# A graph network's edge loops: TensorE's sums wait for VectorE's use of the newest product

## The reference, cut to what matters

```python
# L0, convolution (node_h, w1, we, ...)
h = node_h @ w1.T + b1
msg = silu(h[src] + (edge_attr @ we.T + be))
agg = segment_sum(msg, dst, num_segments=N)
...
# L2, heads
score = einsum('ehd,ehd->eh', K[src], Q[dst]) / sqrt(D)     # clipped to -5..5
ex = exp(score - smax[dst]); denom = segment_sum(ex, dst)
m = V[src] * (ex / denom[dst])[:, :, None]
wV = segment_sum(m, dst, num_segments=n)
```

## Time and profile before

| | us |
|---|---|
| median of 3 runs | 6399.58 (6374.36 to 6405.38) |
| profiled execution, its own time | 6349.92 |
| its span | 6348.1 |
| convolution loop in the span | 88 to 1415 |
| heads loop in the span | 3266 to 4680 |
| mean granted clock of TensorE, whole span | 0.731 of 2.4 GHz |

### The profile page before, as it was taken

How to read it: one execution, slowest core, us unless ns; L and a number is a source line. 1 busy time by engine, 2 the same in 40 slices (tenths; PEclk the granted TensorE clock), 3 DMA queues, 4 the chain that set the end, 5 groups by cost and what they waited for, 6 DMA issues and landing times. The chain is left out here.

```text
span 6348.1 us, 91535 instructions
## 1 busy us (share of the span) xinstructions
PE 4079.3 (64%) x19917; PEld 3572.8 (56%) x19918; DVE 2966.6 (47%) x8050; ACT 1654.5 (26%) x2996; POOL 3411.3 (54%) x3536
## 2 busy tenths in 40 slices
PE   4444444456888787787854344444458888878887
PEld 3444444445777776776744334443347677767665
DVE  5444444456333333335755455455464444444455
ACT  0011110113222222226832222222233333333331
POOL 3565555543656566666635555555535555555550
PEclk6777667666555555558976776666679999999999
DMA  4232222225222222226733333333334444444441
GB/s 103 79 83 81 79 80 80 81 66 114 81 80 80 80 80 80 81 78 173 205 100 97 94 99 96 98 95 94 99 104 126 132 132 137 129 128 134 133 131 48
DMA packets 491156, 645.54 MB, mean 102 GB/s; under 512 B 94519, under 2 KB 354059, under 8 KB 490798
## 3 DMA queue, kind: packets, MB, share of 16 engines
q0 software_dynamic: 132032, 325.99, 17.8%
q1 hardware_dynamic: 346462, 312.02, 17.7%
q10 hardware_dynamic: 12560, 6.52, 0.6%
HBM read 554.38 MB, written 89.82 MB: 101 GB/s over the span
## 5 line engine op out<-in xcount | busy, mean ns | idle before, releaser
L1608 POOL DMA_INDIRECT R<-table_ps,r_idx x832 | 802.8, 965 | 718.3 <-DVE r_idx L1682 377.1
L1389 POOL DMA_INDIRECT R<-table_kv,h_idx x832 | 800.5, 962 | 686.8 <-DVE h_idx L1461 383.0
L1194 POOL DMA_INDIRECT by_src<-R,p_idx x832 | 827.9, 995 | 621.3 <-issue 237.3
L660 POOL DMA_INDIRECT R<-table,c_idx x784 | 747.6, 954 | 568.0 <-DVEq L755 281.1
L1418 PE MATMUL psum<-R,h_oh 128*128 128x137 f32 x1664 | 364.3, 384 | 788.8 <-DVE R L1529 754.3
L692 PE MATMUL psum<-R,c_oh 128*128 x1664 | 354.9, 380 | 689.0 <-remote 201.7
L1418 PEld LDWEIGHTS psum<-R,h_oh 128*128 128x128 f32 x1664 | 321.5, 277 | 820.7 <-DVE R L1529 770.8
L692 PEld LDWEIGHTS psum<-R,c_oh 128*128 128x128 f32 x1664 | 303.3, 273 | 738.9 <-issue 738.8
L1743 DVE TENSOR_TENSOR R<-R,psum 128x256 f32 x832 | 343.2, 413 | 735.9 <-remote 386.8
L1630 PE MATMUL psum<-w_L_gnn_re_w,r_ea 128*128 128x256 f32 x1664 | 555.7, 418 | 202.0 <-DVE X L1722 188.0
L1007 PE MATMUL psum<-R 128*128 x1664 | 439.9, 427 | 175.4 <-issue 170.8
(11 more groups left out here) (339 smaller groups left out, 7763.5 us busy)
## 6 DMA issues: line engine op xcount, KB each, us to landing
R<-by_src SPq DMA_DIRECT2D x220, 260.0 KB, 3.1
r_ea<-in_ea_t SPq DMA_DIRECT2D x832, 64.0 KB
R<-in_ea_t SPq DMA_DIRECT2D x196, 256.0 KB
R<-rel_rows SPq DMA_DIRECT2D x104, 256.0 KB
R<-lo_rows SPq DMA_DIRECT2D x104, 256.0 KB
h_rel<-rel_rows SPq DMA_DIRECT2D x208, 128.0 KB
r_rel<-rel_rows SPq DMA_DIRECT2D x208, 128.0 KB
by_src<-R,p_idx POOLq DMA_INDIRECT x832
```

The costliest lines, as they stand in the source:

```text
L660: g.indirect_dma_start(out=rows[:, u, :], out_offset=None, in_=table, in_offset=bass.IndirectOffsetOnAxis(ap=idx[:, j // GROUPS % 2, u:u + ...
L1194: g.indirect_dma_start(out=by_src, out_offset=bass.IndirectOffsetOnAxis(ap=idx[:, u:u + 1], axis=0), in_=rows[:, u, :], in_offset=None).th ...
L1389: g.indirect_dma_start(out=rows[:, u, :], out_offset=None, in_=table, in_offset=bass.IndirectOffsetOnAxis(ap=idx[:, u:u + 1], axis=0)).the ...
L1608: g.indirect_dma_start(out=rows[:, u, :], out_offset=None, in_=table, in_offset=bass.IndirectOffsetOnAxis(ap=idx[:, u:u + 1], axis=0)).the ...
```

## The change

One wait is added to each of two stages. In the convolution the sum of group n now also waits for `summed` at n + 4, which is `message(n + 1)`. TensorE has just made the product of group n + 1 in the same turn. In the heads the sum of group n also waits for `kq_ready` at n + 5, which is `key_times_query(n + 2)`. Again that is the group whose expansion TensorE made just before in its order. The `min` keeps the last turns, which have no such group, from waiting for ever.

```diff
@@ phase_conv_edges, sum_into_nodes
                     pe.wait_ge(msg_ready, min(n + 1, TILE_GROUPS) if isinstance(n, int) else n + 1)
+                    pe.wait_ge(summed, min(n + 4, TILE_GROUPS + 2) if isinstance(n, int) else n + 4)
                     pe.wait_ge(oh_ready, n + 1)
                     pe.wait_ge(added, G * n + G)
@@ phase_heads, sum_into_nodes
                     pe.wait_ge(msg_ready, n + 1 + GROUPS)
+                    pe.wait_ge(kq_ready, min(n + 5, GROUPS * ITERS + 2) if isinstance(n, int) else n + 5)
                     pe.wait_ge(oh_ready, n + 1)
                     pe.wait_ge(added, G * n + G)
```

## The result

The changed kernel takes 6340.29 us (median of 8 runs, 6323.39 to 6357.52). The kernel before, run beside it, takes 6373.55 (8 runs, 6363.86 to 6405.38). The ratio is 0.9937, 95% interval 0.9917 to 0.9956: faster by 0.63%. The forecast was 6610 and slower. The time lies in the forecast's range of 6250 to 6850, but the sign is wrong.

The account below looks back on a forecast made before the run. Both loops were taken as bound by waits in a cycle of gathers and late TensorE results. Heads +112 and convolution +101 us made +213, on the 6399.6 median 6612, rounded to 6610 us; range 6250 to 6850.

Parts of the forecast that it names:

- What bounds the loops: Convolution and heads: waits, 6.38 and 6.80 us a turn; GpSimd gathers until four buffers are full, then late results come.
- The waits at nothing: TensorE's queue, both loops: 416 added waits of 46 ns, 19 us if unhidden, put at 0 because TensorE idles.
- The lost lead makes runs of eight: Both loops: TensorE's second pair ends too late, so GpSimd stops after eight gathers instead of twelve.
- The pause of 5.89 (heads) and 3.85 to 6.04 (convolution) kept for the shorter runs: GpSimd's pause after a run stays as before, giving 7.8 us a turn in heads and 7.35 in convolution.
- the forecast's own sum: Heads: 9.7 us for eight gathers plus the 5.89 pause, 15.6 us for two turns, 7.8 a turn against 6.80.
- The border at 4.5 us into a run: Both loops: TensorE results ending before 4.5 us into a gather run count at once, later ones come 5 to 11 us late.
- The rival on the other side: Both loops: TensorE's running ahead causes lateness, so the wait removes it; 5800, or about 6200 us if partial; chance 0.22.
- The rule of the Trainium skill: A DMA never contends with a compute engine, so lateness would come from the order of waits and the change could lift it.

Follow-up runs that it names:

- implied waits: Kernel before plus both wait instructions, each one group earlier, where other waits already imply them: 1.0004 on a chip without late results.
- the short lead: Kernel before, no new waits, GpSimd gathering only three groups ahead instead of four: 1.0134 on a chip without late results, 0.998 on one with them.
- the later wait: Against the kernel before: heads' sum waits for the messages of group n + 1 instead of `key_times_query(n + 2)`, convolution unchanged: 0.996 with late results.
- direct transfers: Kernel before with both loops' gathers replaced by direct transfers of as many bytes from fixed places, leaving out the choice of rows: 0.8172.

## Why the prediction was wrong, point by point

- **What bounds the loops.** Right for the chip of the result: waits, in a cycle of gathers and late results. The cycle belongs to the kind of chip, though, and no profile on record at the forecast could show that.
- **The waits at nothing, 416 in TensorE's queue.** Right as far as tested: 1.0004 with implied waits, on a chip without late results.
- **The lost lead makes runs of eight.** Half right: 64 of eight and 57 of four in the heads, but 137 of four and only 20 of eight in the convolution. The sum starts 0.2 us after `key_times_query` and the clock fell from 0.68 to 0.65, both as forecast.
- **The pause of 5.89 (heads) and 3.85 to 6.04 (convolution) kept for the shorter runs.** This is the term that failed, and it carried the sign. Means of 3.33 after eight gathers and 1.81 after four were measured, 3.23 and 1.70 in the convolution. With these the forecast's own sum gives (9.7 + 3.33) / 2 = 6.5 us a turn for a run of eight and 4.7 + 1.81 = 6.5 for one of four, in place of 7.8; the runs of twelve had (14.7 + 5.58) / 3 = 6.8. I had taken the pause for a property of the gathers. It is a fixed 3.27 us and the time for which the result stays away beyond the run's end, and the second fell from 2.31 us to 0.06 and below. A likely reason, argued and not shown, is the number of results outstanding when a run ends: three in the kernel before (an expansion, a sum and the next expansion, raised at 3937.09, 3937.18 and 3937.27 in the run of the earlier trace rows) and mostly one with the wait. (Two slips in the forecast's sum cancel: by its own terms the heads lose 1.00 us a turn and not 0.98, the convolution 0.94 and not 0.97.)
- **The border at 4.5 us into a run.** In the heads of the kernel before it holds: 2 of the 20 expansions that ended 3 to 4 us into a run were late, and all 136 that ended later in one. But it is no property of the gathers. Expansions that ended 2 to 4 us into a run were nearly all late with the short lead, and none was with the later wait.
- **The rival on the other side**, lateness by TensorE's running ahead. Half right: fewer results are late without TensorE's lead (0.86 with it, 0.49 and 0.03 with the two waits), but half of them still are with the change, and it takes indirect gathers as well (none late without). Its 5.0 us a turn in the heads and 5.3 in the convolution had none late as their condition, so they didn't come. On the chip without late results the same waits gave 5.12 and 5.21 (both loops counted in 208 turns), close to the rival's sums.
- **The rule of the Trainium skill**, "SBUF — State Buffer", section "Who interferes with whom". What I made of it (lateness from the order of waits, lifted by the change) had the right sign. That page of the Trainium skill states that a DMA never contends with a compute engine. On the two chips with 5030 us the trace agrees with it, with no late result. On the others the order of waits is the same and results are late, so the order alone is not the cause; yet nothing here shows a contention for the buffers themselves, for the direct transfers, as many bytes to the same places, delay nothing.
- **Noise.** The heads' -34.4 us in the profiles is confirmed: -82.8 on the second chip, and -25.8 between two kernels of the third. The convolution's -15.4 is not settled. It was -26.6 on the second chip, -12.3 on the fourth and -2.1 on the third, always the same way, but untouched loops moved by up to 21.5 us, and alone its wait gave 1.001 (0.9989 to 1.0032).

What is shown: late results need indirect transfers and a chip of one kind, and TensorE's lead makes more of them; on such a chip GpSimd's own semaphore updates stall too. That TensorE's results are late because their updates stand in the same line is argued from this, not shown. It would have to be a line in which VectorE and ScalarE do not stand, since their raises are on time. Open: what in the chip makes the difference, whether two updates or plain waits between gathers would do, and what updates in all four loops give; the kernels for these ran where nothing is late.

## What to carry to other kernels

Where a cycle is made of work and a pause, ask what the pause is made of before keeping it for a cycle of another length: here one part was a fixed chain of 3.27 us, and the other, the time for which a result stayed away beyond the run, went from 2.31 us to 0.06. Before tuning the order of waits around a wait that looks too long for its cause, time the kernel on a second chip: this change gave 0.5 to 1.7% in three comparisons with late results, and cost 2.5% without (its two parts on one chip, with the updates on another). The version to keep is the one with GpSimd's six updates after each gather and no new wait: 0.9751 with late results, on one chip, and, with the updates in all four loops, 1.000 without.

## What was not expected of the hardware

The same program took 5030 us on two chips and 6339 to 6402 elsewhere, with the same 0.95 us for each gather and the same 17 ns for the median semaphore update. On one of the slower ones an update of GpSimd takes up to 1.44 us while indirect gathers run. In the kernel before, TensorE's raise for an expansion comes 6.84 us after its matmuls on the mean, while VectorE's and ScalarE's come within 0.4 us in 96 to 99% of the cases recorded. With direct transfers of the same bytes TensorE's come at once too, at 4.0 and 3.6 us a turn; GpSimd's six updates were not tried there.
